# Three first-half convolution products and the first-half step products of a state-space layer, reordered on TensorE

## What is computed

```
x = x + _L0_ffn_ref(_L0_cond2_ref(x, ...), w1, g1, w2, g2, w3, g3)
x = x + _L1_attn_ref(_L1_cond_ref(x, ...), in_proj_w, conv_w, conv_b, dt_bias, A_log, D, ...)
...
proj = hidden_states @ in_proj_w.T                    # 256 -> 512 gate, 768 xBC, 64 dt
xp = jnp.pad(xBC, ((0, 0), (K - 1, 0), (0, 0)))
conv = conv_b + sum((conv_w[:, i] * xp[:, i:i + l, :] for i in range(K)))    # K = 4
xBC = jax.nn.silu(conv)
dt = jax.nn.softplus(dt + dt_bias)
y = _ssd(x * dt[..., None], dt * A, Bm, Cm)
```

## Time and profile before

| what | value |
|---|---|
| time, median of 3 runs | 692.53 us (692.39 to 693.21) |
| time of the profiled execution | 689.73 us |
| its span, from the first to the last instruction | 687.9 us |
| TensorE busy | 541.2 us, 79% of the span |
| VectorE busy | 407.4 us, 59% |
| ScalarE busy | 373.0 us, 54% |
| GpSimd busy | 147.5 us, 21% |
| mean granted TensorE clock | 0.905 of full speed |

### The profile page before, as it was taken

How to read it: one execution, slowest core, us unless ns; L and a number is a source line. 1 busy time by engine, 2 the same in 40 slices (tenths; PEclk the granted TensorE clock), 3 DMA queues, 4 the chain that set the end, 5 groups by cost and what they waited for, 6 DMA issues and landing times.

```text
span 687.9 us, 13927 instructions
## 1 busy us (share of the span) xinstructions
PE 541.2 (79%) x5668; PEld 392.5 (57%) x5668; DVE 407.4 (59%) x612; ACT 373.0 (54%) x794; POOL 147.5 (21%) x115
## 2 busy tenths in 40 slices
PE   0097769778687766578999999999649999999980
PEld 0054445556455642353664656667648999996560
DVE  5889999999997477966655544454831111111223
ACT  6987788978876407555657555666322222222112
POOL 1000000000000127732019555520021222223110
PEclk9995699878868999899999999999759999999995
DMA  9500000000001000000000000000269999888825
GB/s 350 189 1 1 1 1 1 2 1 1 1 1 32 1 0 1 0 1 1 2 2 2 3 2 2 3 2 3 69 256 423 420 420 361 333 330 304 338 95 191
DMA packets 18480, 71.38 MB, mean 104 GB/s; under 512 B 4849, under 2 KB 9969, under 8 KB 14705
## 3 DMA queue, kind: packets, MB, share of 16 engines
q1 hardware_dynamic: 15408, 64.20, 24.5%
q0 software_dynamic: 1920, 5.25, 2.0%
q10 hardware_dynamic: 1088, 1.05, 0.5%
HBM read 65.77 MB, written 4.72 MB: 102 GB/s over the span
## 4 chain that ended last, share of the span: by engine, by line
PE 52%; DVE 31%; ACT 8%; issue 4%; DMA 3%; POOL 1%; SPq 0%; ACTq 0%; DVEq 0%; POOLq 0%
PE PS L1442 39%; DVE arena L942 4%; DVE nmx L1029 4%; DVE arena L939 4%; PE PS L1948 2%; PE PS L2017 2%; PE PS L1724 1%; PE PS L1589 1%; DVE R L956 1%; DVE arena L953 1%; DVE arena L954 1%; DMA arena<-in_moe 1%; DVE arena L948 1%; DVE arena L949 1%; ACT arena L773 1%
## 5 line engine op out<-in xcount | busy, mean ns | idle before, releaser
L1442 PE MATMUL PS<-arena 128*128 128x128 f32 (+6 forms) x1376 | 156.9, 291 | 17.6 <-DVE arena L1126 11.4
L1442 PEld LDWEIGHTS PS<-arena 128*128 128x128 f32 (+4 forms) x1376 | 125.8, 164 | 41.9 <-issue 25.0
L611 ACT ACTIVATE arena<-PS,nmx 128x128 f32<-128x128 f32 (+1 forms) x128 | 52.0, 422 | 32.6 <-DVE nmx L1029 32.6
L1390 DVE TENSOR_TENSOR R<-arena,PS 128x128 f32<-128x128 f32 x16 | 4.6, 288 | 88.1 <-ACT arena L870 88.1
L389 POOL TENSOR_SCALAR arena<-ident,gcol 128x128 f32<-128x128 f32 x4 | 2.4, 602 | 220.2 <-DMA gcol<-in_gcol 220.2
L449 POOL TENSOR_TENSOR arena<-arena 128x1024 f32<-128x1024 f32 x16 | 37.8, 2367 | 40.6 <-DVE arena L1208 32.5
L1506 PE MATMUL PS<-arena 32*128 32x128 f32 (+1 forms) x128 | 22.9, 438 | 29.9 <-ACT arena L611 29.6
L481 POOL DMA_INDIRECT ypair<-arena,oid x20 | 19.8, 988 | 121.8 <-ACT arena L876 121.8
L1442 PE MATMUL PS<-arena,R 128*128 128x256 f32 x192 | 44.2, 380 | 0.6 <-ACT arena L876 0.6
L1442 PEld LDWEIGHTS PS<-arena,R 128*128 128x128 f32 x192 | 35.2, 190 | 5.1 <-issue 1.0
L942 DVE TENSOR_TENSOR_SCAN arena<-dmat,arena 128x1023 f32<-128x1023 f32 x16 | 37.6, 2348 | 0.6
(11 more groups left out here) (306 smaller groups left out, 1198.3 us busy)
## 6 DMA issues: line engine op xcount, KB each, us to landing
arena<-in_moe SPq DMA_DIRECT2D x23, 1408.0 KB, 8.2
arena<-in_moe SPq DMA_DIRECT2D x23, 768.0 KB, 9.7
inproj<-in_inproj SPq DMA_DIRECT2D x1, 1344.0 KB, 10.5
arena<-in_fT SPq DMA_DIRECT2D x1, 1024.0 KB, 5.0
xT<-in_xT SPq DMA_DIRECT2D x1, 1024.0 KB, 5.4
R<-in_w1T SPq DMA_DIRECT2D x1, 1024.0 KB, 7.4
R<-in_w2T SPq DMA_DIRECT2D x1, 1024.0 KB, 9.4
R<-in_w3T SPq DMA_DIRECT2D x1, 1024.0 KB, 11.5
```

The lines of the kernel that those rows point to most:

```text
L611: sc.activation(pr[u % 2][:, j, 0:n], PS[:, 2 * (u % 2) + j // 2, (j % 2) * 256:(j % 2) * 256 + n], ACT.Exp, bias=nmx[:, u % 2, j:j + 1], ...
L1442: last = mm(dst, l, r, start=(n == 0), stop=(n == len(pairs) - 1))
```

## The change

TensorE's program is reordered in three places, and one wait of ScalarE gets another number. `steps_in(0)` moves ahead of `down(7)`. `conv_half(1, 0)` and `conv_half(2, 0)`, which stood behind `steps_in(1)`, move ahead of the wait for half 1 of `A`, behind `turn_out(7)`. Since the halves are now counted in another order (all three first halves, then the three second halves), `conv_start(n)` of the first three blocks waits for a count of n + 4 and not of 2n + 2. No instruction is added or removed.

```diff
             def conv_start(n):
 
-                act.wait_ge(S["pe_xbc"], 2 * n + 2)
+                act.wait_ge(S["pe_xbc"], n + 4 if n < 3 else 2 * n + 2)
...
+                if s == NT + 4:
+                    steps_in(0)
                 if 0 <= s - 5 < NT:
                     down(s - 5)
                 if s == NT + 4:
-                    steps_in(0)
                     conv_half(0, 0)
 
+            conv_half(1, 0)
+            conv_half(2, 0)
             pe.wait_ge(S["dve_A"], 6)
             steps_in(1)
 
             def conv_in(n):
-                for ch in range(1 if n == 0 else 0, NCH):
+                for ch in range(1 if n < 3 else 0, NCH):
                     conv_half(n, ch)
```

## The result

The changed kernel took 683.58 us (median of four runs, 683.32 to 684.61) where 687.2 was forecast and the range ended at 685.5. The ratio of the first comparison is 0.989, with a 95% interval of 0.9861 to 0.9919. Of the three first halves in the title, two were moved (four of the ten products behind the wait); `conv_half(0, 0)` stands behind `down(7)` as before.

A forecast was written before the change was run, and what follows sets the result against it. TensorE was taken to bound the kernel, with a 3.15 us hole ahead of `steps_in(1)`. The gain 0.42 + 3.43 + 1.70 - 0.17 = 5.38 us gave 692.53 - 5.38 = 687.2 us, range 685.5 to 690.5.

The forecast's parts named there:

- The stretch: TensorE's time from the start of `turn_out(6)` to the first sum of decays; the sum said 5.38 us less.
- The earlier `turn_out(7)`: With `steps_in(0)` ahead of `down(7)`, `turn_out(7)` starts 0.42 us earlier, and half 1 of `A` with it.
- Eight records: The two first halves moved into TensorE's hole ahead of `steps_in(1)`: 3.43 us, less 0.17 for ending after half 1.
- The clock term: Without the hole, no four records at the low clock behind `steps_in(1)`: 1.70 us saved.
- The covers of `out_rows(7)`, `dve_dt` and VectorE's block 4: Slack hiding other engines' work: 1.1 us for `out_rows(7)`, 0.84 for `dve_dt`, 0.7 at VectorE's block 4.
- the last one: Whole kernel: the 5.38 us gain taken from the timed median 692.53, 2.80 above the profiled execution, giving 687.2.
- one of the prediction's own signs of being wrong: A shift of 5 us at 320 us that is smaller at the end of the convolution or of the span.
- The rival without the clock term: Records behind the hole: fewer at low clock before, or as many after; gain 3.68 us, time 688.9; chance 0.18.
- The rival in which the halves run at the low clock: The eight moved records take 6.82 us at the low clock; 2.0 us gained, time 690.5; chance 0.06.
- the slower one: Low clock lasting over 13 or more of the twenty records; up to 3.1 us lost, 695.6; chance 0.03.
- the one with a wait for `dve_dt`: Ahead of the sums of decays, TensorE waits for a late `dve_dt`; gain comes back, about 692; chance 0.06.
- The one with more than forecast: Timed runs of before lose more to the low clock; VectorE caps the gain at 7.0 us, 685.5; chance 0.03.

The follow-up runs named there:

- e2: The changed kernel again, unchanged, timed in turn with the kernel before: 684.33 us, ratio 0.9924 to before.
- e6: The changed kernel with four uncounted identity products added long before the place of the change: 680.47 us, ratio 0.9857 to the kernel before.
- e12: The changed kernel with twelve uncounted identity products added: 680.70 us, ratio 0.9859 to the kernel before.
- e3: The kernel before with only the two first halves moved ahead of the wait, `steps_in(0)` left behind `down(7)`: 685.10 us, ratio 0.9916.
- e4: The kernel before with the hole filled by two uncounted repeats of `conv_half(0, 0)`, no work moved: 684.63 us, ratio 0.9909.
- e9: A further profile of the kernel before, unchanged, one run: 20.82 us from `turn_out(6)` to the first sum of decays.
- e11: One more profile of the kernel before, unchanged, one run: 20.82 us from `turn_out(6)` to the first sum of decays.
- e1: The kernel before again, unchanged, against itself: 690.51 us, ratio 1.000.
- e5: The kernel before with four uncounted identity products added long before the place of the change: 686.77 us, ratio 0.9942.
- e7: The kernel before with only `steps_in(0)` moved ahead of `down(7)`, the halves as before: 690.40 us, ratio 0.9994.

## Why the prediction was wrong

**The place was right, term by term.** The stretch fell by 5.56 us (5.38 forecast), to 15.28 or 15.29 in each of four profiles (the changed kernel, e2, e6, e12). The earlier `turn_out(7)` is worth 0.47 at the end of the stretch (0.42), by e2 against e3. Eight records left the path, and `steps_in(1)` starts right behind them without idle. The clock term of 1.70 is shown by e4, which removes nothing but the hole. The covers of `out_rows(7)`, `dve_dt` and VectorE's block 4 held.

**The step that failed is the last one: "The median lies 2.80 above that execution, and I carry the same gain over: 692.53 - 5.38 = 687.2."** The 692.53 was not a level from which 5.38 could be taken, as the later runs of the kernel before show. In the three later comparisons the kernel before was timed 57 times, besides three profiled executions of e9 to e11: the 60 range from 688.34 to 692.66 with a median of 690.6, and three of them reach 692.39, the lowest of the first three runs. So the median of three stood 1.9 us above the kernel's own, and the profiled execution's 689.73 was nearer to it. From 690.6 the same gain gives 685.2. Three runs that all lie in the top twentieth of the later ones are hardly chance; what set them high stays open, since no run was made to tell (the later comparisons ran on three chips, with medians of 690.28, 691.08 and 691.0; the chip of the first three is not on record). The range was built around the shift at the place and had no term for the level it was taken from, though its own table showed two levels 2.8 apart.

**What is left, 1.6 us from 685.2 to 683.58, is open.** e2 took 684.33, and its gain of 3.7 to 6.9 us holds 5.4. Against the profiled execution the prediction had 684.3, and the profiled execution of the changed kernel took 683.52; that it came so near is partly luck. Of the 6.2 us by which its span is shorter, 1.32 lie ahead of the change and 5.56 in the stretch, and 0.7 were lost behind it. So one of the prediction's own signs of being wrong was there, a shift that is smaller at the end of the span than at the sums of decays. The change did not cause it as far as the profiles tell: the two stalls add up to 3.19 and 3.59 us in the two profiles of the changed kernel and to anything from 2.68 to 3.69 in the five of the kernel before, and the start of `turn_out(6)`, with the same program ahead of it, differs by up to 4.4. No run here shows that the change itself gains anything outside its stretch.

**The rivals.** The rival without the clock term rested on the Trainium skill (TensorE: Matmul & The Clock Gate, section "What's actually happening"), by which the number of products at the low clock varies from run to run. The traces agree on the number: in the first profile four records of 128x512 went by at the low clock, in e1 about three and a part of `steps_in(1)`. But the price does not vary with it at this place, in the order of before: six profiles (before, e1, e5, e9 to e11) have a stretch of 20.82 to 20.85, and a hole of 3.15 in each. In e7, with the same hole, the price is another, with a stretch of 21.79. The rival in which the halves run at the low clock, the slower one and the one with a wait for `dve_dt` were seen in no profile. The one with more than forecast, by a dearer low clock in the runs of before, was not seen either; the time passed its bound of 685.5 by the level, not by the clock.

## What to carry to other kernels

Measure a local change between two fixed rows of the program, and keep that gain apart from the level of the timed runs, which three runs made at one time need not show: here the gain was forecast to 0.2 us and the time missed by 3.6. When work is moved into a hole of TensorE, count the clock behind the hole too, and close it wholly: in the one profile with a rest of 1.43 us, that rest still cost the clock term. And when an experiment adds or drops instructions, look at the whole trace before its time is put down to the edit, since four useless products made both kernels some 4 us faster.

## What the hardware showed that I had not expected

TensorE stood still for 1.05 to 2.06 us, twice, in the same two passes of `within`, behind the 122nd and the 119th of 128 records of small products, with nothing in the profile that it waited for, in every kernel with no TensorE instructions added (before, changed, e1 to e3, e7 to e11). Eight records of matrix products and their weight loads more, at the place (e4) or 55 us ahead of it (e5, e6), took the first stall away and left 0.29 to 0.38 of the second; twenty-four more left none (e12). The two kernels with four added products gained by ratio 4.0 and (e6 against e2, in different comparisons) about 4.6 us.

That the cause is the supply of instructions is not shown by an experiment of its own, but two things in the traces point there. The place of the second stall goes with the number of instructions ahead of it: 4243 weight loads precede the one that ends it in all thirteen profiles that have it, the eight added ones of e4, e5 and e6 counted. That is why it stands behind the 111th record there (17 are left in the row, where 9 were) and not behind the 119th. And a transfer of 16 KB in the queue that the page calls `q8 instruction` ended 1.2 to 1.6 us before each of the 23 stalls did. In the kernel before, the one ahead of the first stall shows in the last two columns (share of the DMA engines, GB/s) of this microsecond, in which the row of small products begins:

```profile
382.00:383.00 1.00, 1.00 (x88) 1.00 (x83) 0.43 (x1) 1.00 (x3) 0.66 (x1) 1.00 0.06 16
```

That TensorE waited for that transfer is not shown, nor why more instructions ahead shorten the stalls. The changed kernel with four such products, at 680.47 us, is the best of all that ran, and e12 with 680.70 can't be told from it.
